# Two graph-attention layers on one core: the second chunk's casts in one step, the third chunk's load behind them, and weight casts moved within their steps

## The reference, cut to what matters

```python
# layer 0: q = x@Wq + bq, k = x@Wk + bk, v = x@Wv + bv, per head
scores = q @ k.T / sqrt(32) + beta * adj
scores = where(adj > 0, scores, -9e15)
x = layernorm(x + softmax(scores) @ v)
# layer 1: no bias on q and k
a = q @ k.T * 384**-0.5 + adj
x = layernorm(x + (softmax(a) @ v) @ Wo.T + bo)
```

## Time and profile before

| | |
|---|---|
| median of three runs | 1102.79 us (1102.42 to 1103.21) |
| the profiled execution's own time | 1102.04 us |
| its span, first to last instruction | 1100.2 us |
| PE busy | 1061.6 us (96% of the span) |
| DVE busy | 936.5 us (85%) |
| POOL busy | 529.2 us (48%) |
| ACT busy | 445.3 us (40%) |

### The profile page before, as it was taken

How to read it: one execution, slowest core, us unless ns; L and a number is a source line. 1 busy time by engine, 2 the same in 40 slices (tenths; PEclk the granted TensorE clock), 3 DMA queues, 4 the chain that set the end, 5 groups by cost and what they waited for, 6 DMA issues and landing times.

```text
span 1100.2 us, 38267 instructions
## 1 busy us (share of the span) xinstructions
PE 1061.6 (96%) x16896; PEld 916.5 (83%) x16896; DVE 936.5 (85%) x1642; ACT 445.3 (40%) x713; POOL 529.2 (48%) x454
## 2 busy tenths in 40 slices
PE   6789999999999999999999999999999999999975
PEld 5678888888888888888888888888888888888864
DVE  4468998989989898898989989898998989878786
ACT  4334434433444344444434344343343434444321
POOL 0235554554545445364554645455364544655443
PEclk9899999999999999999999999999999999999998
DMA  8211211202111111211201111111211210010101
GB/s 271 64 40 36 74 31 49 60 20 61 38 43 59 43 38 46 65 38 43 59 30 51 46 40 56 42 42 42 65 38 43 59 41 11 17 36 2 36 29 37
DMA packets 61749, 53.32 MB, mean 48 GB/s; under 512 B 35984, under 2 KB 55440, under 8 KB 61584
## 3 DMA queue, kind: packets, MB, share of 16 engines
q1 hardware_dynamic: 60752, 49.69, 15.3%
q10 hardware_dynamic: 832, 1.18, 0.3%
HBM read 38.28 MB, written 12.58 MB: 46 GB/s over the span
## 4 chain that ended last, share of the span: by engine, by line
PE 90%; DVE 4%; issue 2%; ACT 1%; DMA 1%; POOL 1%; ACTq 0%; POOLq 0%; DVEq 0%
PE ps_u L346 53%; PE ps_s L363 9%; PE ps_o L346 8%; PE ps_p L431 7%; PE ps_p L446 7%; PE ps_x L376 3%; PE ps_o L460 2%; DVE probs L628 1%; POOL probs L766 1%; DMA k_sb<-in_wk 1%; DVE row_sum L678 1%; DVE xt_lo L656 1%; ACT probs L553 0%; DMA xt_in<-in_x_t 0%; DVE row_max L638 0%
## 5 line engine op out<-in xcount | busy, mean ns | idle before, releaser
L766 POOL TENSOR_TENSOR probs<-probs,row_max 128x768 f32<-128x768 f32 x128 | 209.8, 1639 | 314.9 <-DVE row_max L638 314.9
L772 POOL TENSOR_TENSOR probs<-probs,row_inv 128x768 f32<-128x768 f32 x128 | 188.9, 1475 | 127.1 <-DVE row_inv L686 69.2
L522 ACT COPY probs_t<-ps_p 128x768 f32<-128x768 f32 x128 | 102.7, 802 | 201.9 <-PE ps_p L431 201.8
L346 PE MATMUL ps_u<-w_hi_v,xt_lo 128*128 128x384 f32 x384 | 137.9, 359 | 5.0 <-DVE v_sb L671 5.0
L553 ACT ACTIVATE probs<-probs 128x768 f32<-128x768 f32 x128 | 108.3, 846 | 83.5 <-POOL probs L766 83.4
L678 DVE TENSOR_REDUCE row_sum<-probs 128x12 f32<-128x768 f32 x128 | 121.5, 949 | 23.9 <-ACT probs L553 23.1
L787 POOL TENSOR_TENSOR rstd<-var_eps,minus_half 128x1 f32<-128x1 f32 x128 | 70.3, 549 | 125.5 <-DVE var_eps L719 125.5
L346 PE MATMUL ps_u<-w_hi_v,xt_hi 128*128 128x384 f32 x384 | 129.7, 338 | 0.0
L346 PE MATMUL ps_u<-w_lo_v,xt_hi 128*128 128x384 f32 x384 | 129.3, 337 | 0.0
L346 PE MATMUL ps_u<-xt_hi,w_lo_k 128*128 128x512 f32 x288 | 119.1, 414 | 4.9 <-DVE v_sb L671 4.9
L346 PE MATMUL ps_u<-xt_hi,w_lo_q 128*128 128x512 f32 x285 | 121.7, 427 | 1.7 <-ACT q_sb L541 0.9
(11 more groups left out here) (78 smaller groups left out, 2031.3 us busy)
## 6 DMA issues: line engine op xcount, KB each, us to landing
x_in<-in_x SPq DMA_DIRECT2D x16, 768.0 KB, 4.6
out<-z SPq DMA_DIRECT2D x64, 192.0 KB, 1.9
xt_in<-in_x_t SPq DMA_DIRECT2D x15, 768.0 KB, 4.6
adj<-in_adj SPq DMA_DIRECT2D x64, 128.0 KB, 2.9
xt_in<-in_x_t SPq DMA_DIRECT2D x3, 256.0 KB, 4.7
q_sb<-in_wq ACTq DMA_DIRECT2D x3, 192.0 KB, 4.9
k_sb<-in_wk ACTq DMA_DIRECT2D x1, 576.0 KB, 7.9
v_sb<-in_wv SPq DMA_DIRECT2D x1, 576.0 KB, 7.7
```

Source lines behind the costliest of these rows:

```text
L346: last = nc.tensor.matmul(dst, a(g), b(g), start=(g == 0 and n == 0), stop=(g == KT - 1 and n == 2))
L522: nc.scalar.copy(probs_t[:].rearrange("p (a i) n -> p a (i n)", a=2), ps_p[:, :, 0:KT * P]).then_inc(probs_t_ready, 1)
L766: nc.gpsimd.tensor_tensor(s, s, over_keys(row_max[p]), ALU.subtract).then_inc(shifted, 1)
L772: nc.gpsimd.tensor_tensor(s, s, over_keys(row_inv[p]), ALU.mult).then_inc(probs_ready, 1)
```

## The change

The second chunk's four high parts (ACT) and four low parts (DVE) are all made in step 1 of turn -1, on ACT ahead of that step's q2 and k0 copies. SP issues the third chunk's load directly behind the first bias row, with its wait for the second chunk's last low part, and the loads of v1, x, q1, the other two bias rows, k1 and o1 come behind it. The first bias row gets a semaphore of its own. The weights v1, q1, k1, o1 keep their steps on ACT, (0,0), (0,2), (1,0), (1,2), but stand ahead of `heads_out`; their low parts move one step later on DVE, to (0,1), (0,3), (1,1), (1,3), behind `bias_and_max`. The constants go ahead of `weights_lo("k0")`, the first bias tile goes from step 3 to step 2 of turn -1, and in every step DVE does the first unit's copy ahead of `activations_lo` and `residual` rather than behind them.

```diff
+        w_hi_at = {(0, 0): "v1", (0, 2): "q1", (1, 0): "k1", (1, 2): "o1"}
+        w_lo_at = {(0, 1): "v1", (0, 3): "q1", (1, 1): "k1", (1, 3): "o1"}
...
-            for dst, row in ((bv_rows[0], bv0), (bv_rows[1], bv1), (bo_rows, bo1)):
-                sp.dma_start(dst[:], row.rearrange("(o n) -> o n", o=1).partition_broadcast(P)).then_inc(rows_in, 16)
+            load_row(bv_rows[0], bv0, row_in)
+            load_xt(2)
+            load_w("v1")
             load_x(0)
-            for n in ("v1", "q1", "k1", "o1"):
-                load_w(n)
+            load_w("q1")
+            load_row(bv_rows[1], bv1, rows_in)
+            load_row(bo_rows, bo1, rows_in)
+            load_w("k1")
+            load_w("o1")
...
             first_activations_hi()
             for s in STEPS:
-                if (s.phase, s.t) == (-1, 0):
+                place = (s.phase, s.t)
+                if place == (-1, 0):
                     weights_hi("k0")
+                if place == (-1, 1):
+                    for t in range(TILES):
+                        activations_hi((*ORDER[1], t))
                 if s.turned and s.phase >= 0:
                     activations_hi(s.turned)
...
                 for unit in s.units[1:]:
                     unit_out(unit)
-                if s.turned and s.phase < 0:
-                    activations_hi(s.turned)
+                if place == (-1, 1):
+                    weights_hi("v0")
+                if place in w_hi_at:
+                    weights_hi(w_hi_at[place])
                 if s.prev:
                     heads_out(s.prev)
-                for name in w_at.get((s.phase, s.t), []):
-                    if name != "k0":
-                        weights_hi(name)
...
             first_activations_lo()
             for s in STEPS:
-                if (s.phase, s.t) == (-1, 0):
+                place = (s.phase, s.t)
+                if place == (-1, 0):
+                    constants()
                     weights_lo("k0")
-                    constants()
-                if (s.phase, s.t) == (-1, 3):
+                if place == (-1, 1):
+                    for t in range(TILES):
+                        activations_lo((*ORDER[1], t))
+                    weights_lo("v0")
+                if place == (-1, 2):
                     make_bias0(0)
                 if s.cur:
                     bias_and_max(s.cur)
+                if place in w_lo_at:
+                    weights_lo(w_lo_at[place])
                 if s.done:
                     normalise(s.done)
-                if s.turned:
+                for unit in s.units[:1]:
+                    unit_out(unit)
+                if s.turned and s.phase >= 0:
                     activations_lo(s.turned)
                 if s.last:
                     residual(s.last)
-                for unit in s.units[:1]:
-                    unit_out(unit)
                 if s.cur:
                     sums(s.cur)
                 for unit in s.units[1:]:
                     unit_out(unit)
                 if s.prev:
                     heads_lo(s.prev)
-                for name in w_at.get((s.phase, s.t), []):
-                    if name != "k0":
-                        weights_lo(name)
```

More of the change, by code:

```diff
@@ L190, in two_gnn_layers_kernel @@
         small_in = sem("small_in")
+        row_in = sem("row_in")
         rows_in = sem("rows_in")
@@ L250, in two_gnn_layers_kernel @@
                  "q1": as_weight(x1[1]), "k1": as_weight(x1[2]), "v1": as_weight(x_in[1]), "o1": w_stage[:]}
-        w_at = {(-1, 0): ["k0"], (-1, 1): ["v0"], (0, 0): ["v1"], (0, 2): ["q1"], (1, 0): ["k1"], (1, 2): ["o1"]}
+        w_hi_at = {(0, 0): "v1", (0, 2): "q1", (1, 0): "k1", (1, 2): "o1"}
+        w_lo_at = {(0, 1): "v1", (0, 3): "q1", (1, 1): "k1", (1, 3): "o1"}
         w_count = {n: k + 1 for k, n in enumerate(["k0", "v0", "v1", "q1", "k1", "o1"])}
@@ L311, in _, with load_row @@
             load_adj0(0)
-            for dst, row in ((bv_rows[0], bv0), (bv_rows[1], bv1), (bo_rows, bo1)):
-                sp.dma_start(dst[:], row.rearrange("(o n) -> o n", o=1).partition_broadcast(P)).then_inc(rows_in, 16)
-            load_x(0)
-            for n in ("v1", "q1", "k1", "o1"):
-                load_w(n)
+            def load_row(dst, row, done):
+                sp.dma_start(dst[:], row.rearrange("(o n) -> o n", o=1).partition_broadcast(P)).then_inc(done, 16)
+            load_row(bv_rows[0], bv0, row_in)
+            load_xt(2)
+            load_w("v1")
+            load_x(0)
+            load_w("q1")
[3 more added lines that the diff above has]
+            load_w("o1")
             for s in STEPS:
@@ L325, in _ @@
                 of = s.phase + 1
-                if s.t == 0 and of < N_TURNS and ORDER[of][0] == 0 and 1 <= ORDER[of][1] < CHUNKS - 1:
+                if s.t == 0 and of < N_TURNS and ORDER[of][0] == 0 and 2 <= ORDER[of][1] < CHUNKS - 1:
                     load_xt(ORDER[of][1] + 1)
@@ L666, in unit_out @@
                 if V_NO[unit] == 1:
-                    dve.wait_ge(rows_in, 16 * 3)
+                    dve.wait_ge(row_in, 16)
+                if (layer, c, n) == (1, 0, 0):
+                    dve.wait_ge(rows_in, 16 * 2)
                 user = last_user((layer, c))
@@ L779, in add_bo @@
                 if second_no(tile) == 1:
-                    pool.wait_ge(rows_in, 16 * 3)
+                    pool.wait_ge(rows_in, 16 * 2)
                 rows = x1[c % 3][:, t, :]
```

## The result

The changed kernel takes 1082.51 us (median of four runs, 1081.61 to 1083.73), the kernel before 1103.0 beside it: ratio 0.9823, 95% interval 0.9811 to 0.9835. It is 20.5 us faster. The early turns came out nearly as worked out; 5.9 us came from a stretch for which the prediction took 0.

The account below looks back on a forecast made before the run. PE's work was taken to bound 119.77 to 1000 us, leaving gains only in turns -1 to 2, mostly waits for v copies; 14.6 + 0.65 = 15.3 us less gave a median of 1087.5 us, range 1085.8 to 1091.3.

Parts of the forecast that it names:

- The v copy ahead of `residual`, in 30 turns: Steady part: the residual moves by one 0.5 us copy, with 3 us of cover; gain taken as 0.
- The marker given for it: Any PE idle time between 119.77 and 1000 us was to speak for the copy costing time in the steady part.
- first scores to turn 1's q0: Turn 0: 35.7 us where it was 50.3, so 14.6 us less, 2.8 of them the lower clock.
- turn 2: DVE, no longer behind after o1's low part in step (1,3), gives PE 0.65 us; bounds 0 and 1.1.
- tail: End of the kernel: taken as it is, no gain.
- The load's issue and landing: Third chunk's load: issued at 18.0 us instead of 25.48, landing at 22.1 to 24.5, off the path.
- q2's copy behind the casts: Turn -1: q2's copy waits for four casts, starts at 17.1 us, k1 can start at 17.8; net gain 0.
- POOL gets in first: Steps (0,1), (0,3), (1,3): POOL's shift starts before the low parts, costing 3.7 us; 1091.2 us, chance 0.13.
- the late load: Third chunk's load lands late after all, each us from 25.5 on costing one; 3 us late gives 1090.5 us, chance 0.04.
- the slower one: Steady part: the 0.55 us copy ahead of the residual costs as much in 29 turns; 1103.5 us, chance 0.04.
- the clock rival: Turn -1: PE idling some 1.1 us between k0 and k1 lowers the clock, costing 2.8 us; 1090.3 us, chance 0.05.
- a stall of 0.5 for turn 1's q0: Start of turn 1: PE waits 0.5 us for v2's copy, ready 9.3 us after the scores, wanted at 8.8; bounds 0 and 1.

Follow-up runs that it names:

- e3_copy_between: The kernel before, with only the first unit's copy on DVE moved between `activations_lo` and the residual: 1098.06 us, ratio 0.9955.
- e5_lo_in_gaps: The changed kernel with low parts of v1, q1, o1 behind `sums` and k1's at the end of (0,2), casts earlier: 1079.64 us, ratio 0.9790.
- e7_load_and_copy: The changed kernel with the weights' casts and low parts back at the ends of their steps, load and copy order kept: 1083.26 us, ratio 0.9825.
- e4_load_only: The changed kernel's turn -1 and load order, with the weights' places and the first unit's copy as in the kernel before: 1096.67 us, ratio 0.9941.
- e2_copy_last: The changed kernel with the first unit's copy back behind `activations_lo` and the residual: 1095.52 us, ratio 0.9932.

## Why the prediction was wrong, and where it was right

The failed step is "The v copy ahead of `residual`, in 30 turns", with "but PE has no idle time to give back. I take 0". The copy's use of POOL's hold was named there; what failed is the bound, read from PE's busy time in the earlier trace rows, so that neither the sum nor the range held a gain there. It gave 5.9 us, shown from four sides: the order alone has it, taking the order out takes it away, a copy that lies just behind the hold does not have it, and a pad of the same length gives it back or not by its place. The residual's distance to `result` was the wrong distance too: what was late was POOL's scale, which stands behind `sums`. The marker given for it, PE idle time after 119.77 us, did not show it: that was 0.02 us with the waits there.

The Trainium skill, "Perfetto Trace Analysis", section "Identifying the Most-Contended Engine", says that a matmul's busy share is no good measure of how near TensorE is to its limit, since its instructions are pipelined. The trace agrees: 100% busy in both kernels, 5.9 us apart. PEld's waits name the engine that was late. They are not the whole price: in e3_copy_between two such rows add up to 7.8 us, in before to 6.0, with odd turns of nearly the same length, since in before the 0.1 us by which q0 is late stands in no row. The price is in the lengths from scores to scores.

The terms of the sum:

| term | forecast | measured |
|---|---|---|
| first scores to turn 1's q0 | 14.6 | 13.95 |
| turn 2 | 0.65 | -0.5 |
| odd turns 3 to 27 | 0 | 5.9 |
| tail | 0 | 1.15 |
| all | 15.3 | 20.5 |

*Right.* The load's issue and landing; q2's copy behind the casts (k1 at 17.73, forecast 17.8), though q2 itself started at 13.36 and not at 12.6, which cost nothing; the scores of (0,1), (0,2) and (0,3) at 31.66, 39.70 and 49.17, forecast 31.7, 39.8 and 49.3; DVE ahead of POOL in all four places, with low parts of 1.35 us and shifts of 2.52 beside them (forecast 1.4 and 2.9). The rivals "POOL gets in first" and the late load fall with that, and so does the slower one; the clock rival's condition never came, as PE was idle 0.1 us ahead of k1 and not 1.1.

*Mis-sized: step (0,3).* The working gave `normalise` behind the low part 0.4 us. It took 1.64: it ended 0.23 us after POOL's paused shift (54.94 and 54.71), so the shift seems to have gone on first. PE waited 1.04 us for v3's copy, more than the 1 us that the prediction allowed any wait. DVE, POOL and PE:

```profile
52.03 1.35 DVE L625 TENSOR_TENSOR w_lo_q<-x,w_hi_q 128x1152 fp32r<-128x1152 f32 x1
52.19 2.52 POOL L785 TENSOR_TENSOR probs<-probs,row_max 128x768 f32<-128x768 f32 x1 [3.37 <-DVE row_max L651]
53.30 1.64 DVE L657 TENSOR_SCALAR x<-z,mean_var,rstd 128x384 f32<-128x384 f32 x1
54.85 0.55 DVE L686 TENSOR_TENSOR v_sb<-ps_u,bv_rows 128x384 f32<-128x384 f32 x1
55.45 0.44 PE L356 MATMUL ps_u<-w_hi_v,xt_lo 128*128 128x384 f32 x1 [1.04 <-DVE v_sb L686]
```

The forecast had a stall of 0.5 for turn 1's q0 instead, so the total is off by 0.65 only; that one error made up for part of the other is luck. The Trainium skill, "SBUF — State Buffer", section "Who interferes with whom", lists `tensor_scalar` among the operations that can contend with GpSimd for the shared ports, when their operands meet certain conditions. The row agrees: `normalise` is one, and takes 0.47 us in all but three places of the changed kernel, those behind a paused shift. The forecast had counted only the instructions with two SBUF inputs.

*Wrong sign: turn 2.* The low part in (1,3) meets the same `normalise` (1.63 us), so DVE is behind, not 0.65 ahead, and PE waits for the scale in step (2,0). With the low parts moved away, e5_lo_in_gaps has that step 1.45 us shorter. The wait in the changed kernel, 1.26 us:

```profile
93.32 0.87 PE L441 MATMUL ps_p<-ident,probs 128*128 128x128 f32 x6 [1.26 <-POOL probs L791]
```

*Wrong attribution.* The prediction laid the stalls of turn 0 to the weights' parts. With the weights left where they were, e7_load_and_copy has turn 0 in 8.78, 8.55, 9.49 and 8.22 us, together 35.0 as in the changed kernel. With the copy behind the residual turn 0 takes 42.6 us with the weights in their old place (e4_load_only) and 42.5 in their new one (e2_copy_last). So of the 13.95 us by turn 1 the load gave 6.3, the copy's place some 7.6 and the weights' place next to nothing. The sum came out because it was made for the whole new order, the copy's place included; the wrong cause did not show in it.

*The tail* was taken as it is and gave 1.15 us. That is within what its parts vary by from kernel to kernel: the profiled executions here have step (30,3) at 6.1 us or at 7.5 to 7.7, and the last chain's closing "issue" at 5.4 to 7.0. The granted clock goes with the first: 0.77 to 0.78 in the three long steps (30,3), so the lower of its two levels for part of them, and 1.00 in the seven short ones, in all ten behind 15.1 us at 1.00. What decides that was not settled.

## What to carry to other kernels

A matmul engine that the profile shows 100% busy can still be waiting: compare the lengths of a repeating step from start to start, list the waits of its weight loads, and give an edit on a neighbour's chain a gain as well as a loss in the range. Where one engine holds another's next instruction back, put an instruction that the holder does not touch into that time: 0.47 us in 13 places gave 5.9 us here. Before a long instruction is moved beside a shared port, look at the one behind it too, for it may be the one that is blocked.

## What the runs showed of the hardware

`normalise`, one SBUF tensor and two columns, took 0.47 us where it started ahead of POOL's shift, and 1.63 or 1.64 behind a paused one. A shift that started during a low part of 1.35 us lasted 2.52 us in all four places, against 1.48 to 1.64 elsewhere in the changed kernel. The v copy, which reads one tensor in SBUF and one in PSUM, and a `bn_stats`, which reads one in SBUF, took 0.55 us beside POOL's shift.
